# First down products of a two-expert FFN on four TensorE quadrants, expert addresses by a small DMA, one activation with its layout copied by two engines, both instruction orders replaced

## The chip, the cores and the metric

The kernel runs on one NeuronCore of one Trainium2 chip. The metric is the device time of one launch in microseconds (us), 16 batch elements per launch. Engines are TensorE (PE, with its weight loads PEld), VectorE (DVE), ScalarE (ACT), GpSimd (POOL) and SyncE (SP), whose queue only issues DMAs here.

## What is computed

One decoder layer over x of 16 x 256 x 256 in float32, three residual stages, each after a layer normalisation:

```python
x = x + fourier_mix(ln(x))        # k, v, q projections, FFT, cumulative k*v, times conj(q), normed, inverse FFT
x = x + cross_attention(ln(x), ctx_1024)   # 16 heads of 64, causal mask and ALiBi slopes, output projection
x = x + ffn(ln(x))                # two Kronecker mixture layers with an exact GELU between them
# kmoe, top_k = 2 of 64 experts; tokens are rows of 1024 values, 64 tokens per batch element:
logits = x_flat @ W_router.T
vals, idx = jax.lax.top_k(logits, top_k)
probs = jax.nn.softmax(vals, axis=-1)
Y = jnp.einsum('nkoi,nij,nkpj->nkop', A[idx], x_flat.reshape(-1, d_in1, d_in2), B[idx])
out = jnp.einsum('nkop,nk->nop', Y, probs) * scale + bias
```

The up layer takes 32 x 32 tokens to 64 x 64, the down layer 64 x 64 back to 32 x 32.

## The kernel before

Everything is written by hand: one program per engine, and semaphores between them. The steps of all engines stand in one list, `ORDER` (L69), which is run once per turn, 17 times. A step such as `up.2@3` works in turn t on batch element t - 3, so four batch elements are in work at a time: one in the Fourier stage, one in the projections and first attention pairs, one in the last attention pairs and the up router, one in the up and down products. `DRAIN` is a second list for what is left of elements 14 and 15 after the last turn. `run` (L199) gives each engine its own steps in the order of the list, so the list sets the order within each engine, and, by the waits, that of the whole.

Steps that the change touches, by element c:

- **Routing.** `top` (L1154 to L1160) finds two experts per token and writes `place`, the index times the table's step; `gap_up`/`gap_dn` (ACT, L694), `weights` (L1166 to L1176) and the PE step `spread_up`/`spread_dn` (L925) turn probabilities and places into a row spread over all partitions: two diagonals (`route_diag`) times ones, 256 columns of bank G. `keep_up` (L1186, L1191) and `keep_dn` (L1206, L1211) copy the addresses out of G into `offsets`, one run for each chooser, and the probabilities into `pm`.
- **Choosers.** SP (by DMA), POOL, DVE and ACT bring the chosen experts' matrices together (`choose_*`): for up L409 and L483, for down L423. Each loads its addresses into registers first (L395). A down copy moves the 64 x 32 blocks A and B of one expert in one instruction; there are 8 groups of 16 such units per element: 8 units a group by POOL, 4 by DVE, 4 by ACT.
- **Up.** `up.v` (L949, L955) does the first product of pair v into F and the second of pair v-1 into G, in turn on all four 64 x 64 quadrants of TensorE; DVE weighs (L1223) and adds bias (`pre`, L1232) into `h`.
- **GELU.** `gelu` (L703, L708) applies GELU to `h` twice on ACT: four activations of 64 x 1024 into `hT`, a re-laid copy for the down router, then two of 128 x 1024 in place.
- **Down.** `router_dn` waits for `hT`, `logits_dn` (L908) makes the logits. `dn_first.i` (L974) multiplies `h` by B for two groups into bank F, rows 0-63 to partitions 0-63 and rows 64-127 to 64-127, 16 matmuls of 64 x 64 x 64 (32 records in the trace). `dn_weigh` (L1245) weighs all of F in one instruction, `dn_second` (L988) multiplies by A into G, `y_keep` (L1255) copies out, `y_turn` (L1001) and `final` (L1262) finish, `store` (L469) sends the element out.
- **Banks.** P0 and P1 serve `P_USERS` in turn (`turn1 f inverse turn2 k v q`, 18 uses per element); a use waits until the one two before it has been copied out.

Of the kernel before, what the change touches and what calls it, by code (L numbers as in the profile page):

```python
# [1 line left out]

# [47 lines left out]
def at(b, per_batch, k):  # L50

    return b * per_batch + k
# [17 lines left out]
weigh.1@3 exp.5@2 choose_pool.6@3 choose_pool.7@3 pv.3@2 pre.0@3 turn_a.4@2 catch_a.4@2 v_keep.3@2 f.2@1 keep_out.3@2  # L70
score.6@2 up.2@3 cumulate@1 choose_act.8@3 choose_act.9@3 x2_bias@3 load_ctx@1 turn_b.4@2 k.0@1 choose_sync.8@3
scale.5@2 catch_b.4@2 weigh.2@3 pre.1@3 mask.6@2 f_keep.2@1 product_q@1 choose_pool.8@3 choose_pool.9@3 pv.4@2
choose_sync.9@3 cross.1@1 lane.1@1 up.3@3 choose_sync.10@3 choose_act.10@3 exp.6@2 choose_sync.11@3 x1_bias@2 pre.2@3
turn_a.5@2 catch_a.5@2 k.1@1 turn_b.5@2 keep_out.4@2 weigh.3@3 choose_act.11@3 choose_act.12@3 scale.6@2 catch_b.5@2
up.4@3 pre.3@3 choose_pool.10@3 choose_act.13@3 score.7@2 choose_sync.12@3 choose_sync.13@3 choose_sync.14@3
choose_pool.11@3 choose_pool.12@3 choose_pool.13@3 weigh.4@3 pv.5@2 Q@1 k_keep.0@1 turn_a.6@2 keep_out.5@2 catch_a.6@2
mask.7@2 exp.7@2 k_keep.1@1 choose_act.14@3 up.5@3 weigh.5@3 choose_sync.15@3 turn_b.6@2 catch_b.6@2 inverse@1 pre.4@3
up.6@3 pv.6@2 power@1 scale.7@2 turn_a.7@2 catch_a.7@2 pre.5@3 choose_pool.14@3 choose_act.15@3 keep_out.6@2 weigh.6@3
choose_pool.15@3 k.2@1 turn_b.7@2 catch_b.7@2 up.7@3 k_keep.2@1 pv.7@2 pre.6@3 weigh.7@3 keep_out.7@2 up.8@3 pre.7@3
root@1 x1.0@1 ln2_stats.0@1 wo.0@2 wo.1@2 x1.1@1 gelu@3 ln2_stats.1@1 ln2_root@1 load_x ln2.0@1 ln2.1@1 k.3@1 turn2@1  # L80
x2.0@2 x2.1@2 ln3_stats@2 k_keep.3@1 ln3_root@2 ln1_stats ln1_root ln3@2 xnT2@1 router_dn@3 logits_dn.0@3
logits_dn.1@3 logits_dn.2@3 logits_dn.3@3 part@3 fold@3 ln1 top_dn@3 gap_dn@3 weights_dn@3 ln3_turn@2 q.0@1 q.1@1
q_keep.0@1 spread_dn@3 keep_dn@3 score.0@1 ln3_keep@2 mask.0@1 choose_dve.16@3 q_keep.1@1 logits_up@2 choose_act.16@3
top_up@2 choose_pool.16@3 choose_pool.17@3 choose_pool.18@3 choose_pool.19@3 q.2@1 q.3@1 choose_dve.17@3 exp.0@1
scale.0@1 gap_up@2 q_keep.2@1 turn1 choose_dve.18@3 weights_up@2 turn_a.0@1 choose_act.17@3 score.1@1 q_keep.3@1
catch_a.0@1 dn_first.0@3 turn_b.0@1 mask.1@1 choose_act.18@3 choose_act.19@3 spread_up@2 v.0@1 dn_weigh.0@3 keep_up@2
choose_sync.0@2 xnT1 dn_second.0@3 exp.1@1 catch_b.0@1 choose_dve.19@3 score.2@1 dn_first.1@3 v_keep.0@1 scale.1@1
pv.0@1 y_keep.0@3 mask.2@1 dn_weigh.1@3 choose_sync.1@2 choose_sync.2@2 choose_act.0@2 choose_sync.3@2
choose_pool.20@3 choose_act.20@3 choose_act.21@3 choose_act.1@2 turn_a.1@1 choose_dve.20@3 f.0 dn_second.1@3
choose_act.2@2 score.3@1 exp.2@1 choose_act.3@2 choose_dve.21@3 choose_pool.21@3 dn_first.2@3 y_keep.1@3  # L90
choose_dve.22@3 scale.2@1 dn_weigh.2@3 catch_a.1@1 f_keep.0 keep_out.0@1 choose_pool.22@3 choose_act.4@2
# [55 lines left out]
G_USERS = ("logits_up", "spread_up", "up", "router_dn", "spread_dn", "dn_second", "y_turn")  # L147


def chooser(name, layer, b):  # L150
# [1178 lines left out]
```

## Time and profile before

| | us |
|---|---|
| median of 3 runs (lowest, highest) | 1326.86 (1325.89, 1327.83) |
| the profiled execution, its own time | 1330.54 |
| its span, first to last instruction | 1328.8 |
| PE busy | 1227.9 (92%) |
| ACT busy | 1086.9 (82%) |
| DVE busy | 965.7 (73%) |
| POOL busy | 594.2 (45%) |
| mean granted TensorE clock | 0.981 of full |

Busy PE time counts an instruction from its start to its modelled end; matmuls overlap, so a step's cost to PE is better read from its start to the start of the next step. A granted clock of 1.00 is 2.4 GHz, of 0.5 it is 1.2 GHz; values between are means over a stretch.

### The profile page before, as it was taken

The page shows a single profiled execution, that of the slowest core. Times are in us where ns is not written, and L with a number is a line of the kernel's source. Part 1 is how long each engine was busy: PE and PEld are TensorE (multiplying, and loading weights), DVE is VectorE, ACT ScalarE, POOL GpSimd, SP SyncE. Part 2 cuts the span into 40 slices and gives each one's busy share as a digit, 9 for nine tenths or more (in the row PEclk, how much of TensorE's full clock was granted, in tenths as well). Part 3 has the DMA queues.
Part 4 walks back from the last instruction along what each step waited for, and adds up shares of the span by engine and source line. Part 5 has one row for each costly group of instructions (what it writes and reads, how often), then busy time and mean ns, then how long its engine had stood idle before and what let it go on. Part 6 is the DMA issues. An engine that isn't in the chain of part 4 may idle for free.

```text
span 1328.8 us, 52143 instructions
## 1 busy us (share of the span) xinstructions
PE 1227.9 (92%) x16626; PEld 985.8 (74%) x16626; DVE 965.7 (73%) x3677; ACT 1086.9 (82%) x3158; POOL 594.2 (45%) x1846
## 2 busy tenths in 40 slices
PE   7999999999999999999999999999999989987785
PEld 5677787877778787777778777777877777775574
DVE  1466778695978879596877969587786959777554
ACT  2557898898988899898889989798888979888654
POOL 3112446262645536363544636354553625453242
PEclk9999999999999999999999999999999999999798
DMA  9200101010110101010010101001010100101000
GB/s 287 49 17 14 38 10 42 11 42 19 30 31 13 40 14 41 16 37 24 18 39 14 42 11 41 19 19 42 11 42 12 41 19 19 34 13 32 4 25 10
DMA packets 66210, 42.58 MB, mean 32 GB/s; under 512 B 18065, under 2 KB 64786, under 8 KB 65682
## 3 DMA queue, kind: packets, MB, share of 16 engines
q1 hardware_dynamic: 65938, 39.25, 10.7%
q8 instruction: 135, 2.21, 0.7%
q14 instruction: 137, 1.12, 0.3%
HBM read 34.98 MB, written 4.19 MB: 29 GB/s over the span
## 4 chain that ended last, share of the span: by engine, by line
PE 54%; DVE 16%; issue 10%; SPq 10%; ACT 2%; POOL 2%; DMA 2%; DVEq 1%; POOLq 0%; ACTq 0%
SPq L483 9%; PE P L809 5%; PE X L869 5%; PE P L786 4%; PE P L775 4%; PE PT L869 4%; PE PT L832 4%; PE P L762 3%; DVE own L1142 3%; PE F L949 3%; PE X L856 3%; DVE chosen_dn L423 3%; PE S L825 2%; DVE probs L1101 2%; PE G L908 2%
## 5 line engine op out<-in xcount | busy, mean ns | idle before, releaser
L423 POOL COPY chosen_dn<-experts 64x64 f32 x1000 | 222.5, 279 | 214.2 <-issue 146.4
L664 ACT ACTIVATE probs<-probs,neg_max 128x128 f32<-128x128 f32 (+1 forms) x512 | 226.5, 444 | 24.0 <-DVE neg_max L1101 20.7
L409 POOL COPY chosen_up<-experts 32x128 f32 x512 | 182.3, 356 | 116.5 <-POOL chosen_up L409 49.7
L409 ACT COPY chosen_up<-experts 32x128 f32 x528 | 156.0, 296 | 15.5 <-PE G L955 6.2
L1101 DVE CUSTOM_DVE_ANT_0 probs<-S,distance 128x128 f32<-128x128 f32 (+1 forms) x512 | 151.9, 351 | 12.9 <-PE S L825 9.4
L832 PE MATMUL PT<-ident,probs 128*128 128x128 f32 x768 | 135.8, 286 | 10.3 <-DVE probs L1119 7.2
L703 ACT ACTIVATE hT<-h 64x1024 f32<-64x1024 f32 x64 | 127.0, 1984 | 11.3 <-DVE h L1232 9.9
L1119 DVE TENSOR_TENSOR probs<-probs,rinv 128x768 f32<-128x768 f32 x128 | 129.1, 1009 | 4.4
L775 PE MATMUL P<-ctxT,wk 128*128 128x256 f32 x512 | 124.5, 388 | 2.1 <-DVE x L1079 2.1
L786 PE MATMUL P<-wv,ctxT 128*128 128x256 f32 x512 | 122.5, 382 | 0.0
L1108 DVE COPY probsT<-PT 128x384 f32<-128x384 f32 x128 | 71.3, 557 | 70.0 <-PE PT L832 68.8
L832 PEld LDWEIGHTS PT<-ident,probs 128*128 128x128 f32 x768 | 85.9, 141 | 48.8 <-issue 30.5
L809 PE MATMUL P<-xnT,wq 128*128 128x256 f32 x512 | 117.8, 383 | 0.8 <-ACT xnT L612 0.8
L423 ACT COPY chosen_dn<-experts 64x64 f32 x528 | 86.9, 239 | 36.9 <-issue 30.2
L949 PEld LDWEIGHTS F<-chosen_up,own 64*64 64x64 f32 x2048 | 73.4, 135 | 54.5 <-issue 42.2
L949 PE MATMUL F<-chosen_up,own 64*64 64x64 f32 x2048 | 87.1, 223 | 26.9 <-DMA chosen_up<-in_experts_up 16.6
L526 POOL TENSOR_SCALAR var_eps<-moments 128x2 f32<-128x2 f32 x48 | 10.5, 219 | 223.7 <-DVE moments L1027 222.5
L775 PEld LDWEIGHTS P<-ctxT,wk 128*128 128x128 f32 x512 | 96.2, 195 | 14.2 <-DVE x L1079 2.5
L809 PEld LDWEIGHTS P<-xnT,wq 128*128 128x128 f32 x512 | 94.7, 190 | 14.1 <-ACT kT L627 1.1
L786 PEld LDWEIGHTS P<-wv,ctxT 128*128 128x128 f32 x512 | 93.4, 190 | 11.2
L664 ACT ACTIVATION_READ_ACCUMULATOR probs<-probs,neg_max 128x1 f32 x512 | 95.7, 187 | 0.0
L762 PE MATMUL P<-xnT,wf 128*128 128x256 f32 x384 | 93.8, 389 | 0.7 <-ACT xnT L612 0.7
(133 smaller groups left out, 2855.2 us busy)
## 6 DMA issues: line engine op xcount, KB each, us to landing
chosen_up<-in_experts_up SPq DMA_DIRECT2D x992, 16.0 KB, 1.7
x<-in_x SPq DMA_DIRECT2D x16, 256.0 KB, 2.7
ctxT<-in_ctxT SPq DMA_DIRECT2D x16, 256.0 KB, 3.3
out<-x2b SPq DMA_DIRECT2D x16, 256.0 KB, 2.3
experts<-in_experts_up SPq DMA_DIRECT2D x2, 1024.0 KB, 19.8
wk<-in_xWk SPq DMA_DIRECT2D x1, 1024.0 KB
wo<-in_xWo SPq DMA_DIRECT2D x1, 1024.0 KB
wv<-in_xWv SPq DMA_DIRECT2D x1, 1024.0 KB, 7.7
```

Source lines behind the costliest of these rows:

```text
L409: last = copy(to[row:row + D1, n * 2 * F1:(n + 1) * 2 * F1], experts_up[k][:, bass.ds(held[g % loaded(units), unit], 2 * F1)])
L423: last = copy(dst, src.rearrange("p (m c) -> p m c", m=2))
L664: act.activation(probs[:, e % 4, lo:hi], probs[:, e % 4, lo:hi], ACT.Exp, bias=neg_max[:, e % 4, rt:rt + 1], scale=-1.0, accum_out=rsum[:, ...
L703: act.activation(dst, src, ACT.Gelu).then_inc(hT_ready, 1)
L762: mm = pe.matmul(bank[:, half * 256:(half + 1) * 256], wf[:, ct, i, half * P:(half + 1) * P], xnT[:, ct, :], start=(ct == 0), stop=(ct == ...
L775: mm = pe.matmul(bank[:, i * 256:(i + 1) * 256], wk[:, ct, m * P:(m + 1) * P], ctxT[:, ct, :], start=(ct == 0), stop=(ct == CT - 1))
L786: mm = pe.matmul(bank[:, rt * 256:(rt + 1) * 256], ctxT[:, ct, rt * P:(rt + 1) * P], wv[:, ct, j * 256:(j + 1) * 256], start=(ct == 0), st ...
L809: mm = pe.matmul(bank[:, i * 256:(i + 1) * 256], wq[:, ct, m * P:(m + 1) * P], xnT[:, ct, :], start=(ct == 0), stop=(ct == CT - 1))
L832: mm = pe.transpose(PT[:, j * P:(j + 1) * P], probs[:, e % 4, j * P:(j + 1) * P], ident[:, :])
L949: mm = pe.matmul(F[rows, one], own[rows, m * F1:(m + 1) * F1], chosen_up[v % UP_SLOTS][rows, b:b + F1], start=True, stop=True)
L1101: dve.tensor_tensor_reduce(probs[:, e % 4, lo:hi], S[e % 2][:, lo:hi], distance[:, (1 - rt) * P:2 * P], SLOPES[e], TOP, ALU.add, ALU.min, ...
L1119: dve.tensor_tensor(wide, wide, by, ALU.mult).then_inc(probs_scaled, 1)
```

## The change

Five edits are made together.

1. `dn_first`: of the two groups, the first goes to F as before (rows 0-63 to partitions 0-63, 64-127 to 64-127), the second to bank G with the halves crossed, interleaved matmul by matmul. The second group's B block must therefore lie in the other half than its A block: in odd groups `choose_dn` makes two 64 x 32 copies per unit instead of one of 64 x 64. `dn_weigh` is two instructions (F, then G), `keep_dn` copies `pm` in four pieces of 64 x 32 instead of two of 64 x 64, and `dn_second` writes to P0 or P1 instead of G (22 uses per element).
2. Addresses: `place` is an integer tile, and a DMA on SP's queue (`send_up`, `send_dn`) takes it to `offsets`. The second half of `route_diag`, its half of the spreading matmul, and the address copies of `keep_up` and `keep_dn` go. Choosers load their registers from one common layout, the down ones in more, smaller pieces.
3. GELU: two activations of 128 x 1024 in place, then four 64 x 1024 copies to `hT`: two by ACT (`hT_act`), two by POOL (`hT_pool`).
4. `ORDER` and 5. `DRAIN` are other lists. A turn now begins with `spread_up`, `up.0` of its oldest element and ends after `Q` of its newest; `DRAIN` has 30 filler steps `warm` for 40.

The diff's core (of the two lists only the parts that the prediction reads):

```diff
 ORDER = """
...
+...up.7@3 catch_b.7@2 pv.7@2 pre.6@3
+weigh.7@3 ln1_root ln1 q_keep.1@1 score.1@1 up.8@3 exp.0@1 keep_out.7@2 pre.7@3 gelu@3 hT_pool@3 wo.0@2 wo.1@2
+hT_act@3 router_dn@3 logits_dn.0@3 mask.1@1 q_keep.2@1 scale.0@1 exp.1@1 x2.0@2 x2.1@2 ln3_stats@2 ln3_root@2
+x1_bias@1 logits_dn.1@3 logits_dn.2@3 logits_dn.3@3 part@3 fold@3 top_dn@3 send_dn@3 choose_pool.16@3 ln3@2 gap_dn@3
...
+catch_a.1@1 f.0 f.1 turn_b.1@1 choose_act.0@2 f_keep.0 dn_weigh.0@3 scale.2@1 catch_b.1@1 choose_act.19@3
+dn_second.0@3 choose_pool.20@3 f_keep.1 dn_first.1@3 score.3@1 choose_act.20@3 gap_up@2 choose_act.1@2 dn_weigh.1@3
+pv.1@1 dn_second.1@3 choose_sync.0@2 choose_sync.1@2 choose_pool.21@3 choose_pool.22@3 y_keep.0@3 choose_act.2@2
+choose_dve.20@3 turn_a.2@1 f.2 choose_act.3@2 choose_act.21@3 choose_sync.2@2 y_keep.1@3 choose_act.4@2 f_keep.2
...
-P_USERS = ("turn1", "f", "inverse", "turn2", "k", "v", "q")
+P_USERS = ("turn1", "f", "inverse", "turn2", "k", "v", "q", "dn_second")
...
+                if flip:
+                    copy(to[(1 - half) * F1:(2 - half) * F1, a:a + D1], experts_dn[:, bass.ds(held[i % loaded(units), unit], D1)])
+                    last = copy(to[half * F1:(half + 1) * F1, b:b + D1],
+                                experts_dn[:, D1:][:, bass.ds(held[i % loaded(units), unit], D1)])
+                    continue
...
+            def send(c, layer):
+                groups = (UP_GROUPS, DN_GROUPS)[layer]
+                sp.wait_ge(route_step[layer], at(c, 4, 1))
+                for name in choosers_of(("up", "dn")[layer], 0):
+                    if name != "sync":
+                        after(sp, chosen[name][layer], at(c, groups, 0))
+                to = offsets[layer][:, :].rearrange("p (n k) -> p n k", k=TOPK)
+                sp.dma_start(to, place[layer][:, :]).then_inc(offsets_ready[layer], 16)
...
+            def turn_tokens(c):
+                after(pool, parts_done, c)
+                pool.wait_ge(h_ready, at(c, 2, 2))
+                for oh in range(2):
+                    pool.tensor_copy(*hT_parts(1, oh)).then_inc(hT_pooled, 1)
+                pool.wait_ge(hT_pooled, at(c, 2, 2))
...
-                after(act, parts_done, c)
-                for half in range(2):
-                    for oh in range(2):
-                        src = h[half * F1:(half + 1) * F1, :].rearrange("p (n h o) -> p h o n", h=2, o=F1 // 2)[:, oh]
-                        dst = hT[oh * F1:(oh + 1) * F1, :, half * TOKENS // 2:(half + 1) * TOKENS // 2]
-                        act.activation(dst, src, ACT.Gelu).then_inc(hT_ready, 1)
                 cols = UP_PAIRS // 2 * UP_TOK * F1
-                act.wait_ge(hT_ready, at(c, 4, 4))
                 for i in range(2):
                     part = slice(i * cols, (i + 1) * cols)
                     act.activation(h[:, part], h[:, part], ACT.Gelu).then_inc(h_ready, 1)
...
-                pe.wait_ge(route_ready[layer], at(c, 2, 2))
-                pe.matmul(G[:, 128:384], route_ones[:, :], route_diag[layer][:, :], start=True, stop=True).then_inc(route_spread[layer], 1)
+                pe.wait_ge(route_ready[layer], c + 1)
+                pe.matmul(G[:, 128:256], route_ones[:, :], route_diag[layer][:, :], start=True, stop=True).then_inc(route_spread[layer], 1)
...
-                for j in (0, 1):
-                    g, slot = i + j * DN_PAIRS, (2 * i + j) % DN_SLOTS
-                    for u in range(DN_TOK // 2):
+                for u in range(DN_TOK // 2):
+                    for j in (0, 1):
+                        g, slot = i + j * DN_PAIRS, (2 * i + j) % DN_SLOTS
+                        token, one = g * UP_TOK + u, slice((j * 4 + u) * w, (j * 4 + u + 1) * w)
                         for half in range(2):
...
+                            rows, to = [slice(e * F1, (e + 1) * F1) for e in (half, half ^ j)]
+                            mm = pe.matmul((F, G)[j][to, one], h[rows, token * F1:(token + 1) * F1],
                                            chosen_dn[slot][rows, A_DN + u * w:A_DN + (u + 1) * w], start=True, stop=True)
...
-                take_g("dn_second", i, c)
+                bank = take_p("dn_second", i, c)
...
+                for j, (bank, kept) in enumerate(((F, f_kept), (G, g_kept))):
+                    part, by = slice(j * n * F1 // 4, (j + 1) * n * F1 // 4), slice(i * n + j * n // 2, i * n + (j + 1) * n // 2)
+                    dve.tensor_tensor(W_dn[:, part].rearrange("p (s w) -> p s w", w=D1),
+                                      bank[:, part].rearrange("p (s w) -> p s w", w=D1),
+                                      spread(pm[1][:, by], 2, D1), ALU.mult).then_inc(kept, 1)
```

## Rows read from the trace of the kernel before

**Rows 1.** The stretches view: us, busy time of PE, PEld, DVE, ACT, POOL, granted clock, DMA.
```profile
core 0: us, PE busy (x) PEld busy (x) DVE busy (x) ACT busy (x) POOL busy (x), PEclk, DMA share, GB/s
591.30:667.71 76.41, 73.30 (x1028) 58.98 (x1027) 60.13 (x229) 67.46 (x197) 37.53 (x116) 1.00 0.09 27
...
210.52:1129.86 919.34, 882.21 (x12313) 709.46 (x12313) 718.41 (x2737) 806.53 (x2342) 449.44 (x1392) 1.00 0.10 27
```
**Rows 2.** The same view, the two stretches of the drain.
```profile
1204.82:1275.41 70.59, 50.34 (x811) 39.91 (x811) 41.05 (x160) 48.21 (x137) 26.50 (x97) 0.83 0.06 17
1275.41:1326.18 50.77, 34.86 (x722) 31.18 (x716) 25.49 (x97) 28.30 (x81) 14.63 (x61) 0.90 0.05 13
```
**Rows 3.** The timeline of PE, 638 to 651: start us, us, step, shapes, records.
```profile
641.94 1.11 PE L974 MATMUL F<-chosen_dn,h 64*64 64x64 f32 x32
642.98 0.55 PE L832 MATMUL PT<-ident,probs 128*128 128x128 f32 x3
643.37 0.60 PE L925 MATMUL G<-route_diag,route_ones 128*128 128x256 f32 x2
643.80 1.89 PE L786 MATMUL P<-wv,ctxT 128*128 128x256 f32 x8
```
**Rows 4.** The timeline of PE, one `up` step: first and last of its 16 rows.
```profile
604.58 0.27 PE L949 MATMUL F<-chosen_up,own 64*64 64x64 f32 x2
604.60 0.27 PE L955 MATMUL G<-chosen_up,W 64*64 64x64 f32 x2
...
605.05 0.22 PE L955 MATMUL G<-chosen_up,W 64*64 64x64 f32 x2
605.10 0.40 PE L822 MATMUL S<-kT,qT 64*64 64x128 f32 x8
```
**Rows 5.** The timeline of ACT, then of PE, around GELU of one turn.
```profile
618.90 8.02 ACT L703 ACTIVATE hT<-h 64x1024 f32<-64x1024 f32 x4
626.95 2.01 ACT L708 ACTIVATE h<-h 128x1024 f32<-128x1024 f32 x2
...
617.90 3.72 PE L869 MATMUL X<-wo,attnT 128*128 128x256 f32 x16
...
624.91 1.89 PE L775 MATMUL P<-ctxT,wk 128*128 128x256 f32 x8
...
627.17 2.08 PE L908 MATMUL G<-r_dn,hT 128*64 128x64 f32 x64
```
**Rows 6.** The timeline, three choosers copying down units (ACT, POOL, DVE).
```profile
641.85 1.25 ACT L423 COPY chosen_dn<-experts 64x64 f32 x8
...
643.11 1.50 POOL L423 COPY chosen_dn<-experts 64x64 f32 x8 [0.16 <-POOL chosen_dn L423]
...
650.35 1.04 DVE L423 COPY chosen_dn<-experts 64x64 f32 x8
```
**Rows 7.** Groups by line and form, whole span: counts, busy us, mean ns, idle before.
```profile
L423 ACT COPY chosen_dn<-experts 64x64 f32 x528 | 86.9, 239 | 36.9 <-issue 30.2 <-PE G L988 4.8
...
L1223 DVE TENSOR_TENSOR W<-F,pm_up 128x256 f32<-128x256 f32 x128 | 53.2, 415 | 7.4 <-PE F L949 6.4
...
L1255 DVE COPY experts<-G 64x128 f32<-64x128 f32 x128 | 48.6, 380 | 9.4 <-PE G L988 7.1
L1245 DVE TENSOR_TENSOR W_dn<-F,pm_dn 128x512 f32<-128x512 f32 x64 | 44.0, 688 | 3.3 <-PE F L974 2.2
...
L570 POOL TENSOR_TENSOR x1b<-x,out_bias 128x512 f32<-128x512 f32 x16 | 27.6, 1723 | 1.3
...
L558 POOL COPY fourier<-fourier 1x256 f32<-1x256 f32 x32 | 12.4, 387 | 79.0 <-DVE fourier L1052 69.0 <-DVE fourier L1064 9.5 <-POOL fourier L550 0.5
```
**Rows 8.** The chain of waits near the end: start us, us, what.
```profile
1303.44 0.16 DVE place L1160
...
1305.41 0.48 DVE offsets L1206 x4
1305.91 1.50 ACTq L395
...
1309.85 1.98 PE F L974 x32
...
1320.80 1.16 PE F L974 x32
```
**Rows 9.** DMA issues: KB each, median us from issue to landing.
```profile
chosen_up<-in_experts_up SPq DMA_DIRECT2D x992, 16.0 KB, 1.7
...
fourier<-in_b_fourier SPq DMA_DIRECT2D x1, 3.0 KB, 3.4
```

More of the change, by code:

```diff
@@ L69 @@
 ORDER = """
[L70 to L74, printed above, removed]
@@ L80 @@
[L80 to L84, printed above, removed]
@@ L85 @@
[L85 to L89, printed above, removed]
@@ new lines @@
+warm.38@15 warm.39@15 pre.7@15 gelu@15 hT_pool@15 hT_act@15 router_dn@15 logits_dn.0@15 logits_dn.1@15 logits_dn.2@15
+logits_dn.3@15 part@15 fold@15 top_dn@15 gap_dn@15 weights_dn@15 spread_dn@15 send_dn@15 keep_dn@15 choose_act.16@15
+choose_dve.16@15 choose_dve.17@15 choose_dve.18@15 choose_act.17@15 choose_pool.16@15 choose_pool.17@15
+choose_pool.18@15 choose_dve.19@15 dn_first.0@15 dn_weigh.0@15 dn_second.0@15 choose_pool.19@15 choose_pool.20@15
+choose_pool.21@15 choose_act.18@15 choose_act.19@15 choose_dve.20@15 dn_first.1@15 dn_weigh.1@15 dn_second.1@15
@@ L372, in own_parts @@
             return dst[:, k, il], src[:, 1 - half]
-        def share_of(name, layer, b):
-            units = chooser(name, layer, b)
-            return units, units.start * (UP_GROUPS if layer == "up" else DN_GROUPS)
         def choosers_of(layer, b):
@@ L389, in fetch_offsets @@
             layer, g, step = ("up", n, 2 * F1) if n < UP_GROUPS else ("dn", n - UP_GROUPS, 2 * D1)
-            units, first = share_of(name, layer, c)
+            units = chooser(name, layer, c)
             ahead = loaded(units)
@@ L393, in fetch_offsets @@
                 return
-            first += g * len(units)
-            values = nc.values_load_multi_w_load_instructions(
-                offsets[layer == "dn"][0:1, first:first + ahead * len(units)], engines=[kind], min_val=0, max_val=(EXPERTS - 1) * step,
-                skip_runtime_bounds_check_because="an index of one of 64 logits times the table's step")[1]
-            for i, value in enumerate(values):
-                later, unit = divmod(i, len(units))
-                held[later, units[unit]] = value
+            if layer == "up":
+                of = offsets[0][:, :].rearrange("p (g u) -> p g u", g=UP_GROUPS)
+                pieces = [(of[:, g:g + ahead, units.start:units.stop], range(g, g + ahead), units)]
+            else:
+                each, pieces = DN_TOK // 2 * TOPK, []
+                of = offsets[1][:, :].rearrange("p (e j i u) -> p e i j u", e=2, j=2, u=each)
+                for half in range(2):
+                    some = range(max(units.start, half * each), min(units.stop, (half + 1) * each))
+                    for i in range(g // 2, (g + ahead) // 2):
+                        if some:
+                            pieces.append((of[:, half, i, :, some.start - half * each:some.stop - half * each], (2 * i, 2 * i + 1), some))
+            for view, groups, some in pieces:
+                values = nc.values_load_multi_w_load_instructions(
+                    view, engines=[kind], min_val=0, max_val=(EXPERTS - 1) * step,
+                    skip_runtime_bounds_check_because="an index of one of 64 logits times the table's step")[1]
+                for (group, unit), value in zip(itertools.product(groups, some), values):
+                    held[group % ahead, unit] = value
         def choose_up(copy, held, g, units):
@@ L708, in gelu, with turn_tokens @@
                     act.activation(h[:, part], h[:, part], ACT.Gelu).then_inc(h_ready, 1)
+            def turn_tokens(c):
+                after(act, parts_done, c)
+                act.wait_ge(h_ready, at(c, 2, 2))
+                for oh in range(2):
+                    act.copy(*hT_parts(0, oh)).then_inc(hT_ready, 1)
             run({"xnT1": lambda f: xnT_keep(f, 1), "xnT2": lambda f: xnT_keep(f, 2), "f_keep": f_keep, "k_keep": k_keep,
```

194 lines of the change are left out of this document (92 added, 102 removed).

## The prediction

> **What bounds the kernel now.** I read the busy table first, then the stretches between two stores of `out`, which cut the span into turns. Twelve full turns take 919.34 us, 76.6 each, at a granted clock of 1.00 (2.4 GHz) on average [rows 1]. In such a turn PE is busy 73.5 us (882.21 / 12), ACT 67.2, DVE 59.9 and POOL 37.5 [rows 1]. So PE is idle only 3.1 us in a turn: it is the bound, ACT is second with 9 us to spare, and what leaves PE's list shortens a turn unless a wait takes its place. The reader should see that this holds for the turns only. In the drain, 121.4 us long in its two stretches, PE is busy 85.2 us and at a clock of 0.83 and 0.90 [rows 2]: there the chain from router to choosers to products sets the time, and fewer PE columns are worth little. Element c's down layer runs in turn c + 3, so of 16 elements 14 have theirs in a turn (turns 3 to 16) and two in the drain.
>
> **First products on four quadrants.** From the start of `dn_first` to the start of PE's next step is 642.98 - 641.94 = 1.04 us for 32 records of 64 columns, 32 ns each [rows 3]. The nearest row for four quadrants is `up`, with tiles of the same size, half to F and half to G with crossed halves: its 32 records take 605.10 - 604.58 = 0.52 us, 16 ns each [rows 4]. It is the very pattern that `dn_first` gets, so I take it: 4 x 0.52 = 2.1 us less per element. The bounds are 0 (the crossed products don't overlap) and 2.1.
>
> The trace shows in both rows that two row halves write one bank at the same time. The Trainium skill, TensorEngine Tiling (Array Packing), section Restrictions and Gotchas, speaks against the edit: row tiles should write to different PSUM banks and can't access the same bank simultaneously. By that rule pairs to F and pairs to G would each be in series and the step would gain nothing; the rate of `up` contradicts it here.
>
> **Spreading.** Its product of 256 columns takes 643.80 - 643.37 = 0.43 us [rows 3] and becomes one of 128, twice per element. Half would be 0.21; fixed parts may keep it at 0.3. I take 0.15 each, 0.3 per element (0.2 to 0.4). PE thus loses 2.4 us of 73.5.
>
> **GELU.** ACT's four strided activations take 8.02 us and the two dense ones 2.01 [rows 5]. Two strided passes go to POOL; for a copy with the same strides I take the activation's own 2.0 us, so ACT loses 4.0 (bounds: 4.0 and, if a copy is as fast as the dense pass, 6.0). Who waits: before, the router's products could not start before the fourth pass, 626.9, and they start at 627.17, with `wo`, a `k` and `turn2` on PE as cover from 617.90 [rows 5]. In the new list only `wo.0` and `wo.1` stand between `up.8` and `router_dn`: 624.91 - 617.90 = 7.0 us of cover. The chain behind `up.8` is `pre.7` 0.5, two dense passes 2.0, two ACT copies 4.0: 6.5. That fits with 0.5 to spare, if POOL's two copies also fit into 7.0 - 2.5 = 4.5 us. A POOL copy of 1024 elements isn't in the trace. The bounds: 1.5 us each by the 1 x 256 copy (387 ns x 4), 3.4 by the 128 x 512 `tensor_tensor` with two inputs (1723 ns x 2) [rows 7]; if strides cost POOL what they cost ACT (8.02 / 4 against 2.01 / 2, twice), up to 6.9. I take 1.8, nearer the copy, since it too reads one tensor: 3.6 for two, hidden. Behind `hT_pool` in POOL's queue stand `ln3_root` and `x1_bias`, both due only after `wo.1`.
>
> The Trainium skill, GPSIMD Engine Reference, section Engine selection, says that two-input work is about twice as slow there as on VectorE while one-input work is roughly at line rate. By it the copy would cost half of the two-input row, an estimate of 1.7 us; no row of this trace shows such a copy.
>
> **Crossed groups.** Every odd group has two copies for one: 64 extra copies per element, 32 on POOL, 16 each on ACT and DVE. Eight copies take 1.50, 1.25 and 1.04 us [rows 6], 188, 156 and 130 ns each. Of half the size I take 150, 130 and 100 ns (bounds: the full price, and half of it, which makes the extra zero). Extra per element: POOL 32 x (0.300 - 0.188) = 3.6 us, ACT 16 x 0.104 = 1.7, DVE 16 x 0.07 = 1.1. POOL comes to 37.5 + 3.6 + 3.6 = 44.7 of some 75 and stays far from the bound; ACT to 67.2 - 4.0 + 1.7 = 64.9.
>
> **Addresses.** DVE drops half the diagonals and the address copies, about 1.7 us per element, but pays 1.1 for crossed copies, 4 x (2 x 0.415 - 0.688) = 0.6 for the divided weighing [rows 7] and some 0.3 for `pm`: about even. On the path, `place` is written at 1303.6 and the offsets lie at 1305.9, 2.3 us later [rows 8]. The new way has one issue of 0.4 and a landing of 1.7 to 3.4 us [rows 9] (a 16 KB block, and 3 KB in small rows): 2.1 to 3.8. In a turn that is hidden, since the old way there has PE's queue before the spreading product; in the drain it costs -0.2 to +1.5, I take +0.5. `send` waits on SP's queue for `place` and for old copies of its choosers; behind it stand the next element's SP blocks, which need its addresses anyway, and `load_x` stands ahead. The register loads bring the same number of values (1.50 us for 24 on ACT [rows 8]); more pieces may add a few tenths.
>
> **Both lists.** Their worth can't be summed from rows. PE's idle of 3.1 us per turn is the most they can return; a shorter PE list has less cover for the same chains. I let idle grow by 0.4 us. Fill: nothing.
>
> **The sum.** Per turn -2.4 + 0.4 = -2.0, times 14: -28.0 us. Drain: the last element's four first products cost 1.98 twice and 1.16 twice [rows 8], half is 3.1 less; its router starts 2.0 us earlier (6.0 for 8.0 behind GELU); chooser, weighing and address costs give back 1.4 + 0.6 + 0.5. That is -2.6; element 14, partly covered, -1.4. Together -32.0. Against the profiled execution's own 1330.5 this gives 1298.5; its median is 3.7 lower, so I forecast 1326.9 - 32.0 = **1295 us**.
>
> **Rivals.**
> - *Banks P0 and P1 become the wait (0.22).* `dn_second` adds 4 uses to 18, and in the new list `dn_second.0` and `.1` hold both banks until `y_keep.0` (two copies of 0.38 us [rows 7]) runs, with `f.2` behind. For it: POOL's later, doubled copies also delay `dn_first`. Against it: 3 to 5 us of other PE steps between. Price: one exposed `y_keep` of 0.76 and a few tenths elsewhere, 1.1 us per turn: 1295 + 15.4 gives 1310.
> - *POOL's strided copies are the bound (slower, 0.12).* Beyond 4.5 us for both, each microsecond stops PE at `router_dn` in every turn. The forecast is used up at 4.5 + 2.0 + 2.0 / 14, about 6.6 us for both, 3.3 a copy. With a copy of 3.8, just above the two-input row, the stall is 3.1 per turn: 14 x (-2.0 + 3.1) = +15, drain even, giving 1342. Against it: POOL reads one tensor here.
> - *The crossed products don't overlap (0.04).* PE keeps 2.1 x 14 = 29 us: 1326, no change.
> - *The lists also remove idle (0.05).* One more us per turn gone and a shorter drain: 1278.
>
> **How the numbers follow.** The forecast's case (0.57) spans 1282 to 1308: idle grows by 1.3 at most or not at all, the drain moves by 6 either way. The range is 1279 to 1327; it leaves out the slower case and the last one, 0.17. About 0.2% (1324 to 1330) is what a measurement here can tell from no change. Faster: 0.57 + 0.22 + 0.05 = 0.84; same 0.04; slower 0.12.
>
> **What would show it.** In the profile after: PE busy per turn near 71.1 us and turns near 74.6; 0.52 us from `dn_first` to the next PE step; two POOL copies at the `hT` tile of 1.5 to 2.3 us and `logits_dn` within 0.3 us of the end of `wo`; ACT near 65 us per turn; `offsets` landing 2.1 to 3.8 us after `place`. Wrong would be: turns above 75.5 with PE idle over 4.5 (then the waits of `f.2`, `router_dn` or `dn_first` name the rival), or `dn_first` still near 1 us at full clock. A shorter PE list could also let the granted clock in the drain drop below 0.83.

## The result, and the profile after

| | before | after |
|---|---|---|
| median, lowest to highest (us) | 1326.38, 1324.66 to 1327.83 | 1435.29, 1433.55 to 1437.56 |
| span of the profiled execution | 1328.8 | 1431.7 |
| to the first store of `out` | 210.5 | 218.0 |
| twelve turns, first to thirteenth store | 919.3 (76.6 each) | 991.7 (82.6 each) |
| from there to the last store | 196.3 | 219.4 |

The change makes the kernel slower: the ratio of after to before is 1.0823, with a 95% interval of 1.0801 to 1.0845. The forecast of 1295 us and its range, up to 1327, both missed. Between the two profiled executions lie 103 us (109 between the medians), and 72 of them are in the twelve turns, 6.0 in each.

The page of the kernel after, its busy times and its chain of work by engine and line:

```profile
PE 1214.1 (85%) x16586; PEld 952.2 (67%) x16586; DVE 1029.6 (72%) x3903; ACT 1099.0 (77%) x3390; POOL 769.6 (54%) x2378
...
PE 31%; POOL 28%; issue 12%; POOLq 12%; SPq 6%; DVE 4%; DMA 3%; ACT 1%; ACTq 1%; DVEq 0%
POOLq L408 8%; POOL chosen_dn L434 6%; POOL chosen_dn L433 6%; POOL chosen_dn L440 5%; SPq L510 5%; PE P L843 4%; PE X L903 4%; PE PT L903 4%; POOL chosen_up L421 3%; PE F L984 2%; PE G L943 2%; PE X L890 2%; DMA offsets<-place 2%; PE PT L866 2%; POOL fourier L577 1%
```

In the kernel before, this chain was 54% PE and 2% POOL. Now POOL with its queue holds 40% of it. L433 and L434 are the two 64 x 32 copies of an odd group, L440 the 64 x 64 copy of an even one, L408 the loads of addresses into registers. Yet POOL is busy for no more than 54% of the span. The busy table does not give this bound away; the chain does.

The stretches view of after, which answers to [rows 1] (one turn, then twelve) and [rows 2] (the two stretches of the drain):

```profile
630.52:713.15 82.63, 74.48 (x1026) 58.32 (x1027) 63.81 (x242) 66.67 (x207) 49.01 (x151) 0.96 0.09 25
217.97:1209.68 991.71, 875.10 (x12313) 684.51 (x12313) 768.84 (x2904) 815.13 (x2509) 583.25 (x1801) 0.99 0.09 25
1287.77:1368.73 80.96, 54.31 (x899) 43.26 (x899) 46.71 (x183) 51.49 (x160) 39.20 (x139) 0.81 0.06 16
1368.73:1429.04 60.31, 26.91 (x572) 23.56 (x568) 26.37 (x111) 27.72 (x97) 22.42 (x81) 0.64 0.04 10
```

PE is busy 72.9 us of a turn (875.10 / 12), 0.6 less than before, and idle 9.7 instead of 3.1. POOL went from 37.5 to 48.6, where 44.7 had been forecast. The drain is 141.3 us long instead of 121.4, at a granted clock of 0.81 and 0.64 where before had 0.83 and 0.90.

The chain of waits through one turn of after (start us, us, what) shows where a POOL with 34 idle us in a turn can bind:

```profile
663.74 3.45 PE PT L903 x16
667.20 2.04 PE G L943 x64
...
671.12 0.29 DVE top_idx L1195 x2
671.63 1.70 DMA offsets<-place
673.41 1.09 POOLq L408
674.53 1.09 POOLq L408
676.71 0.64 POOL chosen_dn L440 x3
...
689.52 1.08 POOLq L408
690.62 1.08 POOLq L408
...
703.36 0.92 POOL chosen_dn L434
704.32 0.21 POOL chosen_dn L433
704.56 0.22 POOL chosen_dn L434
704.85 0.73 POOL fourier L577
705.58 0.70 POOL fourier L578
...
707.47 1.90 POOLq L408
709.87 0.67 POOL chosen_up L421
...
714.67 0.68 PE F L984 x16
```

From the router's result at 671 to the next element's first `up` at 714.67 the chain runs on POOL and its queue almost without a break: register loads, its 64 down units, the Fourier steps, more loads, its first up units. POOL's idle time lies elsewhere in the turn, where nothing may start: it stands before `hT` until GELU is done, 139.0 us in the 16 elements. Between 671 and 714.67 PE has other steps for a part of the 43 us only. What PE itself waited for, over the whole span (waits view: us in total, times, longest), names ACT's copies too:

```profile
PE F L984 <- POOL chosen_up L421: 22.4, 28, 1.1
PE F L1010 <- ACT chosen_dn L434: 18.6, 5, 9.4
```

The two prices that the forecast got wrong. First the copies, on POOL and on ACT (timeline: start us, us):

```profile
677.50 0.21 POOL L433 COPY chosen_dn<-experts 64x32 f32 x1 [0.16 <-POOL chosen_dn L440]
677.75 0.21 POOL L434 COPY chosen_dn<-experts 64x32 f32 x1
678.00 0.21 POOL L433 COPY chosen_dn<-experts 64x32 f32 x1
...
686.39 0.22 ACT L434 COPY chosen_dn<-experts 64x32 f32 x1
686.62 0.21 ACT L433 COPY chosen_dn<-experts 64x32 f32 x1
686.84 0.22 ACT L434 COPY chosen_dn<-experts 64x32 f32 x1
```

They start 0.25 us apart on POOL and 0.23 on ACT: a unit costs 0.50 and 0.45 us, against 0.188 and 0.156 for a 64 x 64 copy [rows 6]. Then the loads (duration min/median/max in ns), after and, in the second fence, before:

```profile
L408 ACTq TENSOR_LOAD <-offsets x132: 560/1366/3007, 117.6 to 1413.1; - x132
L408 POOLq TENSOR_LOAD <-offsets x128: 1077/1877/2289, 125.2 to 1411.7; - x128
```
```profile
L395 POOLq TENSOR_LOAD <-offsets x96: 561/567/2033, 116.7 to 1311.9; - x96
L395 ACTq TENSOR_LOAD <-offsets x96: 539/548/1497, 117.6 to 1311.0; - x96
```

In a turn POOL has four up loads of 1.88 us where they took 0.57, and four down loads of 1.08 where there were two of 2.03: 11.8 us for 6.3.

### The profile page after: what moved, and what is told of

It reads as the page before. It is cut to its first block, busy times and chain, and to the rows that moved or that the text cites. A ratio compares the mean times of both kernels' runs of the same rounds, so it can differ in the third digit from the quotient of the medians.

```text
span 1431.7 us, 54316 instructions
## 1 busy us (share of the span) xinstructions
PE 1214.1 (85%) x16586; PEld 952.2 (67%) x16586; DVE 1029.6 (72%) x3903; ACT 1099.0 (77%) x3390; POOL 769.6 (54%) x2378
## 4 chain that ended last, share of the span: by engine, by line
PE 31%; POOL 28%; issue 12%; POOLq 12%; SPq 6%; DVE 4%; DMA 3%; ACT 1%; ACTq 1%; DVEq 0%
POOLq L408 8%; POOL chosen_dn L434 6%; POOL chosen_dn L433 6%; POOL chosen_dn L440 5%; SPq L510 5%; PE P L843 4%; PE X L903 4%; PE PT L903 4%; POOL chosen_up L421 3%; PE F L984 2%; PE G L943 2%; PE X L890 2%; DMA offsets<-place 2%; PE PT L866 2%; POOL fourier L577 1%
## 5 line engine op out<-in xcount | busy, mean ns | idle before, releaser
L421 POOL COPY chosen_up<-experts 32x128 f32 x512 | 165.8, 324 | 178.1 <-issue 99.6
L440 POOL COPY chosen_dn<-experts 64x64 f32 x500 | 114.8, 284 | 129.2 <-issue 118.6
L622 POOL COPY hT<-h 64x1024 f32<-64x1024 f32 x32 | 62.1, 1941 | 139.9 <-ACT h L736 139.0
L433 POOL COPY chosen_dn<-experts 64x32 f32 x500 | 115.8, 232 | 28.6 <-POOL chosen_dn L440 10.5
L434 POOL COPY chosen_dn<-experts 64x32 f32 x500 | 116.7, 233 | 20.7
L1156 DVE TENSOR_TENSOR probs<-probs,rinv 128x768 f32<-128x768 f32 x128 | 122.9, 960 | 4.4
L843 PE MATMUL P<-xnT,wq 128*128 128x256 f32 x512 | 122.6, 383 | 0.8 <-ACT xnT L647 0.8
L1010 PE MATMUL F<-chosen_dn,h 64*64 64x64 f32 x1024 | 49.1, 241 | 79.6 <-issue 42.5
L1010 PEld LDWEIGHTS F<-chosen_dn,h 64*64 64x64 f32 x1024 | 41.1, 150 | 96.1 <-issue 96.1
L809 PEld LDWEIGHTS P<-ctxT,wk 128*128 128x128 f32 x512 | 93.2, 191 | 14.7 <-issue 2.3
```

The lines of the kernel that those rows point to most:

```text
L421: last = copy(to[row:row + D1, n * 2 * F1:(n + 1) * 2 * F1], experts_up[k][:, bass.ds(held[g % loaded(units), unit], 2 * F1)])
L433: copy(to[(1 - half) * F1:(2 - half) * F1, a:a + D1], experts_dn[:, bass.ds(held[i % loaded(units), unit], D1)])
L434: last = copy(to[half * F1:(half + 1) * F1, b:b + D1], experts_dn[:, D1:][:, bass.ds(held[i % loaded(units), unit], D1)])
L440: last = copy(dst, src.rearrange("p (m c) -> p m c", m=2))
L809: mm = pe.matmul(bank[:, i * 256:(i + 1) * 256], wk[:, ct, m * P:(m + 1) * P], ctxT[:, ct, :], start=(ct == 0), stop=(ct == CT - 1))
L843: mm = pe.matmul(bank[:, i * 256:(i + 1) * 256], wq[:, ct, m * P:(m + 1) * P], xnT[:, ct, :], start=(ct == 0), stop=(ct == CT - 1))
```

## The experiments

The theory after this reading: POOL's serial chain binds, through the copies and the loads (chooser theory). The main rival: the two P banks, with `dn_second` now among their users (bank theory). All ratios are to the kernel before on the same chip, with their 95% intervals; a difference between two kernels is taken between their ratios, times 1325 us.

### One edit at a time

**quad_only** is the kernel before with edit 1, old lists and old addresses.

```diff
-P_USERS = ("turn1", "f", "inverse", "turn2", "k", "v", "q")
+P_USERS = ("turn1", "f", "inverse", "turn2", "k", "v", "q", "dn_second")
...
+                if flip:
+                    copy(to[(1 - half) * F1:(2 - half) * F1, a:a + D1], experts_dn[:, bass.ds(held[i % loaded(units), unit], D1)])
...
+                            rows, to = [slice(e * F1, (e + 1) * F1) for e in (half, half ^ j)]
...
```

> The kernel before with the first edit alone (four quadrants, crossed odd groups, second products to P0 or P1), old lists. Chooser theory: a crossed unit costs POOL 0.50 us instead of 0.19, ACT 0.45 for 0.16, DVE 0.38 for 0.13, so POOL has 10 us more per turn, ACT 5 and DVE 4, against 2 us less on PE: slower, about 1350 us (1335 to 1370), with dn_first waiting for chosen_dn. List theory (the new lists are what is slow, the edits are good): PE's 2 us per turn come through, 1300 us (1295 to 1310).

Measured: 1426.34 us, 1.0768 (1.0713 to 1.0822). Edit 1 alone loses 102 us, almost the whole loss of the change. The chooser theory had the direction and a quarter of the size (26 us). Nor does POOL hold the time by itself under these lists: the chain that ended last is 42% PE, 13% POOL with its queue and 7% ACT, and PE waited at `dn_first` for copies of all three choosers (30.5 us for POOL's, 17.2 for DVE's, 8.6 for ACT's).

**dma_only** is the kernel before with edit 2 (`place` by a small transfer, loads from the common layout).

> The kernel before with the second edit alone (addresses by DMA from SP's queue, registers loaded from the common layout in pieces), old lists. Chooser theory: POOL's register loads for an up step take 1.9 us instead of 0.57 and ACT's 1.8 instead of 0.55, four of each per turn, 5 us more per turn on either queue: slower, about 1345 us (1332 to 1360). List theory: no change or a little faster, 1318 to 1328.

Measured: 1332.85, 1.0068 (1.0047 to 1.0090): 9 us lost, at the low end of the chooser theory's range.

**gelu_only** is the kernel before with edit 3, POOL's copies right behind `gelu` in the list.

> The kernel before with the third edit alone (two dense activations, then two layout copies on ACT and two on POOL), old lists with the copies right behind gelu. Chooser theory: ACT has 4 us less per turn and the router starts earlier, POOL has slack there: slightly faster, about 1318 us (1308 to 1327). Blocking theory (POOL waits for GELU at the head of its queue and what stands behind it comes late): slower than 1332 us.

Measured: 1342.23, 1.0135 (1.0103 to 1.0167). The waits name a place: DVE stood 91.8 us before `xn` L1047 for POOL's `rstd`, which was queued behind the `hT` copies. **gelu_behind_ln2** puts `hT_pool` behind `ln2_root`:

```diff
-gelu@3 hT_pool@3 hT_act@3 ln2_stats.1@1 ln2_root@1
+gelu@3 hT_act@3 ln2_stats.1@1 ln2_root@1 hT_pool@3
```

> gelu_only (1342) with POOL's two copies behind ln2_root in its queue instead of ahead of it. Blocking theory: ln2's root no longer waits for GELU, so the 18 us come back, and ACT's 4 us per turn may add a little: 1320 us (1312 to 1328). If something else in the edit costs (copies beside ACT's on the same data): 1335 us or more.

Measured: 1333.81, 1.0055 (1.0021 to 1.0089). The wait fell to 35.3 us (32.0 in the kernel before), and the loss from 18 us to 7. The blocking is real and explains 11 of the 18; the other 7 were not followed up. In the kernel after `hT_pool` stands behind `ln2_root` too.

**edits_old_lists** is the kernel after with both old lists, the new steps put in beside their neighbours.

> All three edits under the old lists, with the new steps put in right behind top and gelu. Chooser theory: the edits are slow whatever the list, 1390 us or more (1370 to 1450), near the changed kernel's 1435. List theory: the new lists cost the time, so this is 1330 us or less.

Measured: 1474.04, 1.1136 (1.1103 to 1.1169). The new lists are worth 41 us to the changed kernel, about 11 of which, by the gelu runs, would belong to one step: `hT_pool` stands ahead of `ln2_root` here, as in gelu_only, and DVE's wait for `rstd` is 91.9 us again (11.1 in the kernel after). They hide a part of the edits' price; they don't cause it.

**two_quadrants** is the reverse of quad_only: the kernel after without edit 1.

> The changed kernel with edit 1 undone (two quadrants, one copy per unit, second products to G), new lists, addresses by DMA and the new GELU kept. Copy theory: about 95 us come back, 1340 us (1320 to 1360). If the new lists need the shorter PE steps: 1375 us or more.

Measured: 1344.06, 1.0147 (1.0111 to 1.0183). Edit 1 costs 90 us within the changed kernel as well.

### Why a copy costs 0.25 us

**copies_only** is the kernel before, where an odd group makes two 64 x 32 copies per unit into the same half. Nothing else changes.

```diff
+                if i % 2:
+                    copy(to[half * F1:(half + 1) * F1, a:a + D1], experts_dn[:, bass.ds(held[i % loaded(units), unit], D1)])
+                    last = copy(to[half * F1:(half + 1) * F1, b:b + D1],
+                                experts_dn[:, D1:][:, bass.ds(held[i % loaded(units), unit], D1)])
+                    continue
```

> The kernel before, only that each unit of an odd group is copied by two 64 x 32 instructions, both to the half where the one 64 x 64 copy went. Nothing else moves. Copy theory (two copies of half the size cost what quad_only showed, 0.50 us a pair on POOL): nearly all of quad_only's loss, 1415 us (1390 to 1430). Alternation theory (the copies are slow because they write the two halves of the partitions in turn): a pair takes 0.3 us and the time is 1345 to 1370. Bank theory (the loss is from P0 and P1 and the divided weighing): below 1340.

Measured: 1363.41, 1.0288 (1.0248 to 1.0327), as the alternation theory had it. The number of copies is that of quad_only, and they start closer together. POOL, then ACT:

```profile
652.76 0.21 POOL L422 COPY chosen_dn<-experts 64x32 f32 x1
652.91 0.21 POOL L421 COPY chosen_dn<-experts 64x32 f32 x1
653.06 0.22 POOL L422 COPY chosen_dn<-experts 64x32 f32 x1
...
653.12 0.21 ACT L422 COPY chosen_dn<-experts 64x32 f32 x1
653.24 0.21 ACT L421 COPY chosen_dn<-experts 64x32 f32 x1
653.36 0.21 ACT L422 COPY chosen_dn<-experts 64x32 f32 x1
```

0.15 us apart on POOL, 0.12 on ACT and, in the same trace, 0.09 on DVE (0.19 in the kernel after). One copy lasts 0.21 us in both kernels. In the one that writes the same half, the next starts before the last has ended; in the one that goes from half to half, it doesn't. The Trainium skill, Perfetto Trace Analysis, section Optimizing Scalar/DVE Operations, says that about half of a small operation's latency is the acknowledgement of its write, which overlaps with the next instruction. The copies into one half agree with it (0.12 apart for 0.21 on ACT), those that alternate don't (0.23 for 0.22).

**after_grouped** tests it in the kernel after: the same crossed copies, first all A blocks, then all B blocks, so that the half changes once in a group.

```diff
-            for unit in units:
+            for piece in range(2 if flip else 1):
+                for unit in units:
...
+                    if flip and piece == 0:
+                        last = copy(to[(1 - half) * F1:(2 - half) * F1, a:a + D1], experts_dn[:, at_unit])
+                        continue
+                    if flip:
+                        last = copy(to[half * F1:(half + 1) * F1, b:b + D1], experts_dn[:, D1:][:, at_unit])
+                        continue
```

> The changed kernel with the copies of an odd group in another order: first all A blocks (to one half of the partitions), then all B blocks (to the other), so the halves change once per group and not with every copy. Alternation theory: the copies overlap again, 0.15 us from start to start on POOL for 0.25, 6.4 us less per turn on POOL, 3.5 on ACT: 1390 us (1375 to 1405). Size theory (64 x 32 blocks with crossed halves are slow in any order): no change, 1430 to 1440.

Measured: 1358.45, 1.0236 (1.0195 to 1.0278). The order of the copies alone is worth 78 of the 109 us, more than expected. The share of POOL with its queue in the chain that ended last falls from 40% to 28%. A group's 16 copies now read as follows on POOL, eight in 1.29 us:

```profile
649.43 1.29 POOL L435 COPY chosen_dn<-experts 64x32 f32 x8 [0.16 <-POOL chosen_dn L443]
650.76 1.29 POOL L438 COPY chosen_dn<-experts 64x32 f32 x8
```

**quad_grouped** is quad_only with the copies sorted in the same way.

> A full kernel: the kernel before with edit 1 alone and an odd group's copies sorted by half, old lists. Unsorted it took 1426, with one copy per unit 1350. Theory that alternation between the halves is what makes the extra copies dear: the copies start 0.15 us apart on POOL and 0.12 on ACT again, and 35 to 65 us come off: 1375 (1360 to 1392). Rival, that edit 1's price lies in the number of copies and not in their order: within 15 us of 1426.

Measured: 1372.26, 1.0365 (1.0334 to 1.0395). 53 of quad_only's 102 us are back, under the old lists as well.

### What the copies and the loads cost together

Some kernels leave a part of the computation out, to bound the two costs. **after_free_copies** makes one copy per unit in odd groups, A and B into the same half (the wrong blocks for the crossed products). **contig_loads** reads each chooser's registers as one contiguous piece (many units get another token's expert). **after_free_contig** does both. **quad_free_copies** makes the one copy per unit in quad_only.

```diff
-to, flip = chosen_dn[i % DN_SLOTS], i % 2
+to, flip = chosen_dn[i % DN_SLOTS], 0
```
```diff
+            first = units.start * (UP_GROUPS if layer == "up" else DN_GROUPS) + g * len(units)
+            values = nc.values_load_multi_w_load_instructions(
+                offsets[layer == "dn"][0:1, first:first + ahead * len(units)], engines=[kind], min_val=0, max_val=(EXPERTS - 1) * step,
...
```

> The changed kernel with each chooser's registers loaded in one piece from neighbouring addresses, as before; the addresses are those of other tokens, so other experts are chosen, the number of values is the same. POOL theory (POOL's queue is the bound, 5.5 us of its loads per turn go): 1365 us (1350 to 1385). If the loads lie beside other waits: 1415 us or more.

> The changed kernel with one copy per unit in odd groups too (A and B in the same half, so half the second products take blocks of the wrong place), all else kept, new lists. Copy theory: below the kernel with two quadrants (1344), about 1320 us (1305 to 1335), since PE has 2 us less per turn. Bank theory (P0 and P1 eat PE's gain here too, as under the old lists): 1344 us or more.

> The kernel after with one copy per unit in odd groups (A and B into the same half, so the blocks there are not those of the unit's expert) and with each load of registers one contiguous piece (so many units get another token's expert): both leave the right result. One copy per unit alone gave 1328, a contiguous load alone took 36 us off the kernel after and 22 off the kernel with two quadrants. If register loads are all that hides the shorter PE list, this comes to 1292 to 1308, turns near 74.5 us and PE idle about 2 us per turn. If the two P banks, with dn_second among their users, hold PE, the loads' time is off the critical path here: 1320 or more, with PE's idle time in front of P put down to the copies out of it.

Measured (us, ratio):

| kernel after with | loads in pieces | contiguous loads |
|---|---|---|
| crossed copies that alternate | 1435.29, 1.0823 | 1399.56, 1.0554 (1.0510 to 1.0599) |
| one copy per unit | 1328.04, 1.0020 (1.0003 to 1.0037) | 1290.31, 0.9754 (0.9731 to 0.9776) |

The two prices add: 106 us for the copies down either column (0.0803 and 0.0800 of 1325), 36 and 35 for the loads along the rows. Contiguous loads alone, 1400, lie between the POOL theory's range (1350 to 1385) and its rival's (1415 or more). Each variant frees POOL, DVE and ACT at once. That POOL's part is what counts under the new lists rests on the chain, where POOL with its queue falls to 32% with contiguous loads, 12% with one copy per unit and 1% with both. With both gone the kernel stands 33.2 us under its own before (1323.52), where the forecast said 32.0. Its turns:

```profile
504.58:578.69 74.11, 71.18 (x1026) 56.27 (x1027) 60.50 (x227) 63.51 (x196) 41.03 (x119) 1.00 0.10 28
209.86:1093.75 883.89, 856.94 (x12313) 675.34 (x12313) 728.12 (x2713) 762.74 (x2318) 491.11 (x1417) 1.00 0.10 28
```

73.7 us a turn, PE busy 71.4 and idle 2.3: what the sum forecast for PE is there once POOL's chain is short. It also decides against the bank theory for the new lists, whose condition was 1320 or more.

> quad_only with one copy per unit again: in odd groups A and B lie in the same half, so half the second products take blocks of the wrong place; everything else of edit 1 stays (four quadrants, P banks, divided weighing). Copy theory: PE's 2 us per turn come through or at least nothing is lost, 1300 to 1326 us. Bank theory: still slow, 1345 us or more.

Measured: 1350.36, 1.0195 (1.0157 to 1.0233). Under the old lists 26 us stay lost with one copy per unit, which the bank theory had said. PE and its loads wait for `fourier` to be copied out of a P bank, and PE waits for bank G until `dn_weigh` has read it (waits view: us in total, times, longest), waits that the kernel before doesn't have:

```profile
PEld P L767 <- ACT fourier L624: 22.9, 13, 2.0
PE P L767 <- ACT fourier L624: 21.1, 13, 1.9
PE G L930 <- DVE W_dn L1254: 17.4, 14, 1.4
```

No run changes one of the two banks alone, so what each costs is not shown.

**two_quad_contig** is two_quadrants with contiguous loads (again other tokens' experts).

> The changed kernel without edit 1 and with the registers loaded in one piece (other tokens' experts). If the loads in pieces cost as much here as in the changed kernel (36 us): 1308 us. If they matter only beside POOL's crossed copies: 1335 to 1344 us.

Measured: 1322.38, 0.9971 (0.9951 to 0.9991), between the two theories: the loads cost 23 us here (0.0176), not 36. Beside it, 1290.31 says what the quadrants themselves bring when their copies are free: 0.0217, 29 us.

### Full kernels without the short loads

A load of neighbouring values is cheap and one of scattered pairs dear, so the up addresses should lie as token, group, expert: a chooser's four groups are then eight neighbours. **grouped_runs4** (after_grouped) and **two_quad_runs4** (two_quadrants) lay them out so by four small DMAs:

```diff
-                to = offsets[layer][:, :].rearrange("p (n k) -> p n k", k=TOPK)
-                sp.dma_start(to, place[layer][:, :]).then_inc(offsets_ready[layer], 16)
...
+                to = offsets[0][:, :].rearrange("p (t g k) -> p t g k", t=UP_TOK, k=TOPK)
+                for j in range(UP_TOK):
+                    sp.dma_start(to[:, j], place[0][j:F1:UP_TOK, :]).then_inc(offsets_ready[0], 16)
```

> A full kernel: the kernel after with an odd group's copies sorted by half, and the up addresses laid out by token, group and expert (four small DMAs for one), so that each load of up registers reads runs of eight neighbouring values instead of pairs. Sorting alone gave 1358. Load theory: the up loads on POOL and ACT fall from 1.9 us to 1.2 or less each, and 15 to 30 us come off: 1335 (1325 to 1345). If the four issues on SP's queue or their landing delay the choosers instead, or the loads do not bind once the copies are sorted: 1352 to 1365.

> A full kernel: the kernel after without edit 1 (first down products on two quadrants, one copy per unit) and with the up addresses in runs of eight. Contiguous loads took 22 us off this kernel (1344 to 1322). Load theory: 1325 (1318 to 1332), level with the kernel before. If runs of eight are worth little or the four DMAs cost what they save: 1338 to 1346.

Measured: 1342.48, 1.0151 (1.0123 to 1.0180), and 1336.07, 1.0098 (1.0068 to 1.0127). 11 and 6 us back, less than hoped: the first lies in its range, the second above it. The landing of the four DMAs, each issue 0.58 us, is a wait now:

```profile
L425 ACT COPY chosen_up<-experts 32x128 f32 x528 | 156.1, 296 | 38.9 <-DMA offsets<-place 26.1 <-PE G L1002 3.7 <-issue 1.0
```

**grouped_permuted** and **two_quad_permuted** reach the same layout with the one DMA. The transposes in front of the up router write its tokens in the order token within group, then group:

```diff
-F[:, ct * 256 + rt * P:ct * 256 + (rt + 1) * P]
+F[:, :].rearrange("p (c t g r) -> p c g t r", c=CT, t=UP_TOK, r=4)[:, ct, rt * 8:(rt + 1) * 8]
...
-G[rows, 128:256].rearrange("p (v h n k) -> p h k v n", h=2, n=UP_TOK, k=TOPK)[:, 1 - half, k]
+G[rows, 128:256].rearrange("p (n v h k) -> p h k v n", h=2, n=UP_TOK, k=TOPK)[:, 1 - half, k]
```

`own_parts` and `keep_up` read in the new order.

> A full kernel: the kernel after with the same token order and an odd group's copies sorted by half. Sorting alone gave 1358, with four address DMAs 1342. If their landing was the rest: 1328 (1320 to 1336), and the remaining distance to the 1290 of the kernel with one copy per unit and contiguous loads is the 64 extra copies per element, overlapped. If not: 1340 or more.

> A full kernel: the kernel after without edit 1, and with the up router's tokens in the order token within group, then group, from the transposes on, so that the one small DMA already leaves the up addresses as token, group, expert and each register load reads runs of eight neighbouring values. If the four DMAs' landing was what runs of eight cost before, ACT's wait for the addresses is gone and the time is that of the contiguous load, 1322 (1317 to 1328). If loads in runs of eight are worth little: 1334 or more, as with four DMAs.

Measured: 1325.13, 1.0000 (0.9984 to 1.0015), and 1329.33, 1.0033 (1.0018 to 1.0048). The first is as expected; the second is 1 us above its range. The four DMAs' landing was the rest: by the one DMA the layout is worth 31 and 15 us. grouped_permuted, its loads, then one turn and twelve:

```profile
L412 ACTq TENSOR_LOAD <-offsets x136: 543/562/1379, 120.7 to 1308.7; - x136
L412 POOLq TENSOR_LOAD <-offsets x128: 561/928/2311, 128.2 to 1307.6; - x128
```
```profile
591.21:667.18 75.97, 71.61 (x1027) 56.28 (x1027) 61.95 (x243) 65.37 (x210) 45.54 (x151) 1.00 0.10 27
213.63:1119.77 906.14, 858.78 (x12317) 676.04 (x12317) 741.51 (x2906) 787.29 (x2513) 552.17 (x1801) 1.00 0.10 27
```

Sorted copies and long runs take all 109 us back and end level with the kernel before: turns of 75.5 us instead of 76.6, paid for by 3.1 us more before the first store and 7.0 more behind the thirteenth. No full kernel of this study beats the one before. It stands 33 us (0.0246) above after_free_contig. Contiguous loads would bring some 8 of them, by two_quad_permuted against two_quad_contig (0.0062); the other 25 are the 64 extra copies per element, by what is left and not by a run of their own. POOL with its queue is 7% of the chain here, PE 47%.

## Why the prediction was wrong

**PE's part was right.** `dn_first` takes 0.5 to 0.6 us on four quadrants at a granted clock of 1.00; one of this turn's four ran at 0.50 and took 0.88. First and last of its 16 rows, and PE's next step:

```profile
681.94 0.27 PE L1010 MATMUL F<-chosen_dn,h 64*64 64x64 f32 x2
681.96 0.27 PE L1010 MATMUL G<-chosen_dn,h 64*64 64x64 f32 x2
...
682.41 0.23 PE L1010 MATMUL G<-chosen_dn,h 64*64 64x64 f32 x2
682.57 1.13 PE L796 MATMUL P<-xnT,wf 128*128 128x256 f32 x4
```

So the row held, and not the rule of the Trainium skill, TensorEngine Tiling (Array Packing), section Restrictions and Gotchas, that the prediction set against it. after_free_contig shows that such a gain follows: PE busy 71.4 us per turn (71.1 forecast), turns of 73.7 (74.6). That the medians give 33.2 us beside a sum of 32.0 is in part luck: PE's idle time fell by 0.8 us per turn where the sum let it grow by 0.4, and the two stretches of the drain are 2.3 us shorter, not 4.0. The two profiled executions lie 43 us apart, since that of the kernel before (1330.54) was slower than its median and the other (1288.01) faster.

**GELU was right in size.** POOL's two strided copies take 3.95 us for two, 1.97 each (1.8 forecast), ACT's 3.96, and `logits_dn` starts at 667.20, with the end of `wo` at 667.19. So the slower rival on these copies named the right engine and the wrong work. In the kernel before, though, the edit by itself gained nothing: 18 us lost in gelu_only, 7 in gelu_behind_ln2.

```profile
662.84 3.95 POOL L622 COPY hT<-h 64x1024 f32<-64x1024 f32 x2 [8.37 <-ACT h L736]
```

**The addresses' landing was right, their loads were not.** `offsets` lands 1.6 to 2.4 us after its issue (1.7 to 3.4 forecast). The step that failed is "the register loads bring the same number of values". They do, but the layout, not the number, sets the price: eight values as four pairs take 1.88 us on POOL, as neighbours 0.57. The term was "a few tenths" and is 5.5 us of POOL per turn, and 36 us of the kernel. No row of before could show it, because each load there is one run: 24 values in the 1.50 us of [rows 8], 8 in ACT's median of 0.55. These rows give a price per value (0.06 to 0.07 us) for that layout alone.

**The crossed copies are the main failure.** The step was "of half the size I take 150, 130 and 100 ns", bounded above by the full price of a 64 x 64 copy. POOL's copy cost 250, ACT's 227, DVE's 190: the smaller copy is dearer than the larger one, because [rows 6] are starts of copies into one half, and the new ones change halves every time. copies_only hit the assumption (150 on POOL, 118 on ACT); the alternation broke it. The upper bound was taken from rows that had the overlap, and so was no bound. POOL's extra is 32 x (0.50 - 0.188) = 10 us per element, not 3.6.

**"POOL 44.7 of 75 stays far from the bound"** is the step that hid it. It compared a sum with a turn. POOL's load isn't free to move: its down units can't start before the router and must be done before its first up units. Those 43 us, into which nearly all of the 10 and 5.5 more fall, were the number to set against PE's cover. Nor were the extra copies free on the other engines, even at the assumed prices: copies_only pays 150 ns on POOL and loses 38 us (its chain is 23% DVE, 16% before, and 3% POOL), and with sorted copies some 25 us stay in grouped_permuted.

**The fill and the drain** were wrong as well. The fill, put at nothing, is 7.5 us longer, and the drain, forecast 4.0 shorter, is 19.9 longer. With both prices gone (after_free_contig) they are 209.9 and 119.0 us, for before's 210.5 and 121.4. The warning about the clock in the drain came true, 0.81 and 0.64; what that alone costs is not shown, for after_free_contig has 0.82 and 0.74 and a drain shorter than before's.

**The rivals.** The bank rival (1310) shows as waits under the old lists (21 us in front of `f`) and not under the new ones (0.2 us of PE in all, in the kernel after). No rival was "POOL's chooser chain binds", although its two parts stood among the costs.

**The lists** were held to be worth little beyond PE's idle time of 3.1 us per turn. They are worth 41 us to the changed kernel (some 30 without the place of `hT_pool`, an estimate by the gelu runs), whose PE is idle 10.5 us per turn under the old ones. The new lists without the edits were not run.

What stays open: how the loss divides between POOL's, ACT's and DVE's copies, what the banks cost under the old lists, why a change of halves ends the overlap of two copies (only that it does was shown), and the other 7 us of gelu_only.

## What to carry to other kernels

Price a small instruction by start-to-start time in the very sequence that the change will issue, and take no bound from rows whose neighbours differ. Before calling an engine "far from the bound", measure the window between what releases its work and who waits for it, not its share of the turn. In this kernel the chain of waits showed it (POOL with its queue 40%, before 2%), the busy table (54%) did not. Sort small copies by the partitions that they write, and lay values that are loaded into registers side by side.

## What the runs showed of the hardware

- Two copies in a row overlap if they write the same 64 partitions, and don't if they change halves: 0.15 against 0.25 us from start to start on POOL, 0.12 against 0.23 on ACT, 0.09 against 0.19 on DVE, for 64 x 32 float32.
- A register load costs by runs of neighbouring values: eight in one run 0.57 us on POOL, eight in pairs 1.88, which is 0.23 for each value. The Trainium skill, Runtime: NRT & Kernel Launch, section Instruction fetch mechanics, gives about 200 ns per register even in bulk; the loads that the page means come from HBM. From this on-chip tile the pairs cost that, and the run of eight, at 0.07 per value, does not.
- A float32 copy of 64 x 1024 with strides takes POOL 1.94 us, as long as ACT.
- Products of two row halves into different partitions of one bank, in turn with those into a second bank, start every 16 ns per record in two different steps: `up` (32 records in 0.52 us) and `dn_first` (30 in 0.47, 681.94 to 682.41).
